# Second attention: strides of four query blocks instead of two, one score matmul per head and block, all value products as 64-column tiles

## The chip, the cores and the metric

The kernel runs on one core of a Trainium2 chip. The metric is the time of one execution on the device, in microseconds (us). A run's time is the median of several executions. TensorE (PE) multiplies matrices and writes to PSUM, eight banks of 128 partitions x 512 float32. VectorE (DVE) and ScalarE (ACT) read PSUM and write SBUF; GpSimd (POOL) works on SBUF alone; SyncE (SP) issues the DMAs. Each engine takes its instructions in the order in which they are written, and they meet through semaphores.

## What is computed

Two layers on x of 4 x 1024 tokens x 256. Each is `x + attention(layernorm(x)) * silu(ffn(layernorm(x)))`. The change is in the attention of the second layer alone:

```python
NUM_HEADS, HEAD_DIM, WINDOW, GLOBAL_HEADS = 32, 64, 128, 2
q, k, v = (xn @ W.T, split in 32 heads of 64)           # Wq, Wk, Wv: 2048 x 256
q, k = q * cos + rotate_half(q) * sin, k * cos + rotate_half(k) * sin
# heads 0 to 29, for each block of 128 queries that begins at `start`
ks = max(0, start - 64)
s = q[start:start+128] @ k[ks:start+128].T / 8          # causal mask, softmax
out = softmax(s) @ v[ks:start+128]
# heads 30 and 31: the same over all keys up to the query
return out @ Wo.T + bo
```

So a block of 128 queries of a local head looks at its own 128 keys and at the 64 keys before them: 192 columns of scores, 128 for the first block of a sequence.

## The kernel before, in words

The program has four stages: `first_half`, `first_attention`, `gate_network` and `second_attention`. The last is the one that is changed; in the trace it begins at about 1705 us. All its matmuls are float32 or fp32r.

**Turns and strides.** Two heads lie on 128 partitions, 64 each, and are worked on together in a *turn*; 4 sequences x 16 head pairs are 64 turns. 60 of them are local; the last of each 16 is *whole* (heads 30 and 31, all keys). A local turn has 8 query blocks and goes in 4 *strides* of two blocks; a whole turn has 8 strides of one block. `second_attention_plan` writes one list of steps, `plan`, and every engine walks through it and emits its own part of each step. The order of the list is therefore the order of each engine's instructions.

**The steps of a stride** and the letters used for them here:

- **S** (`first`): PE makes the scores into banks 0 to 3. The two heads use the upper and the lower 64 rows of the array. DVE adds the mask, writes SBUF (`pp`) and takes the row minimum of the negated scores (`nm`), one operation for each block and head; ACT then takes the exponential of each (`b_pp<-b_pp,b_nm`) with its sum.
- `second`: DVE takes the reciprocals of the sums, POOL multiplies the weights by them (`b_pp<-b_pp,b_rc`).
- **T** (`third`): PE transposes the weights of one block, three tiles of 128x128, into a bank; DVE copies them to `pt`, for blocks 1 and 5 ACT does.
- **W** (`fourth`): PE multiplies values by weights into bank 7; after four blocks ACT copies the bank to `oT`.

Before, S of stride s comes with W of stride s-3, `second` of s-1 and T of s-2. For one block the key layout is head 0: own 128 keys, earlier 64 keys; head 1: earlier 64, own 128. So head 0 takes two score matmuls (L1666 and L1669) and head 1 one of 192 columns (L1668). The two sets of 64 earlier keys make one transposed tile together. W is then one full-width matmul with a block-diagonal `vb` of the earlier values of both heads (L1717), and two 64-column matmuls, one a head, with the own values (L1722).

**Work for later turns** lies between: **P** (`proj`), 4 a turn, projects q or k for 512 tokens of the next turn (six 512-column matmuls; ACT copies to `qf`); `cos`, `sin`, `add` make the rotary embedding on DVE and POOL, with the rotated half fetched by DMA; **V** (`values`), 4 a turn, makes 128 tokens of values for the next pair of turns (six 256-column matmuls; ACT copies to `vv`). `w_high` and `v_high` are ACT copies of weights, once a turn and once in two turns. **O** (`out`) is the output projection of 128 tokens (eight records of 256 columns, L1731); DVE adds it to `acc`. Two O's fall in a local turn.

**Banks.** P, T, V and O take banks 4, 5, 6 in rotation, in the order of the plan. So each of them waits until the step three places before it in that order has been read out: T of a stride's second block, the fourth in the row P, T, V, T, waits for ACT's copy of P.

A float32 matmul of the program shows in the trace as two records; transposes and fp32r matmuls show as one.

Of the kernel before, what the change touches and what calls it, by code (L numbers as in the profile page):

```python
# [1234 lines left out]
def second_attention_plan():  # L1235
# [6 lines left out]
    def work(n):  # L1242
# [16 lines left out]
        if 2 * m < NTURN:  # L1259
            for i in range(4):  # L1260

                slot = 2 * i + 1 if n % NP or n == 0 else 5 + i // 2 * 2
                out[slot].append(("values", m, n % 2 * 4 + i))
# [14 lines left out]
    def end(at):  # L1278

        out = [[], [], [], []]  # L1280
        if 0 <= at - 3 < len(strides):
            out[0] = [("fourth", at - 3)]
        if 0 <= at - 1 < len(strides):
            out[1] = [("second", at - 1)]
        if 0 <= at - 2 < len(strides):
            out[2], out[3] = [("third", at - 2, 0)], [("third", at - 2, 1)]
        return out

    for n in range(NTURN):
# [13 lines left out]
        for j in range(8 if last else 4):  # L1303
            strides.append((n, j if last else 2 * j))
            s = len(strides) - 1
            a, c = (slots[j], []) if last else (slots[2 * j], slots[2 * j + 1])
            e = end(s)
            p += [("first", s)] + e[0] + e[1] + a + e[2] + c + e[3]
            if store:
                p.append(store.pop())  # L1310
            if side and s % 2:
                p.append(side.pop(0))
                if p[-1][1] % 4 == 3:
                    store.append(("store", *p[-1][1:]))
# [3 lines left out]
    for s in range(len(strides), len(strides) + 3):  # L1318
        p += [x for y in end(s) for x in y]
# [5 lines left out]
def second_attention(nc, A, M, X, out):  # L1325
    with ExitStack() as ctx:
# [14 lines left out]
        def counts(s):  # L1341

            return 4 * s - 2 * sum(whole(n) for n, _ in strides[:s])
# [3 lines left out]
        slot_of, slot_users, pt_of, pt_end = {}, [], {}, {}  # L1347
        for s in plan:
# [3 lines left out]
            elif s[0] == "first":  # L1352
                n, i = strides[s[1]]

                read = (nm_ready, counts(s[1] + 1))
                if whole(n) and i >= 4:
# [5 lines left out]
                slot_of[s[1]] = [len(slot_users) + h for h in range(2 if whole(n) else 1)]  # L1362
                slot_users += [s[1]] * len(slot_of[s[1]])
# [17 lines left out]
        mk = sb("mk", [128, L + 64])  # L1381
# [8 lines left out]
        qf = [sb(f"qf{i}", [128, L]) for i in range(2)]  # L1390
        rt = [sb(f"rt{i}", [128, L]) for i in range(2)]
        qk = [[sb(f"{n}p{i}", [128, L]) for i in range(2)] for n in "qk"]
        vv = [sb(f"vv{i}", [128, NQ, 256]) for i in range(2)]
        vb = [sb(f"vb{i}", [128, NQ - 1, 128]) for i in range(2)]
        pp = [sb(f"pp{i}", [128, L]) for i in range(6)]
# [4 lines left out]
        nm = [sb(f"nm{i}", [128, 4]) for i in range(4)]  # L1400
        sm = [sb(f"sm{i}", [128, 4]) for i in range(4)]
        rc = [sb(f"rc{i}", [128, 4]) for i in range(4)]
# [5 lines left out]
        rt_in = [[sem(f"rt_in{i}{h}") for h in range(2)] for i in range(2)]  # L1408
# [13 lines left out]
        sins = {s[1:]: i + 1 for i, s in enumerate(s for s in plan if s[0] == "sin")}  # L1422

# [3 lines left out]
        def third_done(s):  # L1427

            return P.filled(("third", s, 1, pieces(s, 1) - 1))

        def n_sums(s):
            return 2 if whole(strides[s][0]) else 4

        def weights(s, u, h):


            lo, hi = span(strides[s][1] + u, h)
            return pp[slot_of[s][0] % 6][:, 384 * u + lo:384 * u + hi]

        def span(i, h):  # L1440

            return (192 * h + (0 if i else 64 * h), 192 * h + (192 if i else 128 + 64 * h))
# [8 lines left out]
        def sync(e):  # L1451
# [7 lines left out]
            w.wait_ge(set_up, 1)  # L1459
            e.dma_start(mk[:, L - 128:L], A["mask"]).then_inc(c_in, 16)  # L1460
            for s in plan:
# [17 lines left out]
                elif k == "earlier":  # L1479
                    v = vv[n // 2 % 2]  # L1480
                    w.wait_ge(*P.emptied(("values", n // 2, NQ - 1)))
                    w.wait_ge(set_up, 5)
                    if n >= 2:
                        w.wait_ge(pv_done, pt_end[vb_before(n)])
                    for h in range(2):
                        at = n % 2 * 128 + 64 * h
# [442 lines left out]
```

## Time and profile before

| | us |
|---|---|
| median of 3 runs | 3341.18 |
| the runs | 3335.10, 3341.83, 3341.18 |
| profiled execution | 3339.75 |
| its span, first to last instruction | 3338.0 |
| share of the span: PE / PE weight load / DVE / ACT / POOL busy | 96 / 68 / 67 / 58 / 38% |

How to read the rows further below. A row of the timeline has the start in us, the time in us, the engine, the line of the kernel, the operation and what it writes and reads. Neighbouring rows of one kind are merged, with their count. Matmuls overlap: the time of one row runs on past the start of the next. What a step takes on PE is therefore the difference of two *starts*. "[1.35 <-ACT b_qf L1583]" is idle time ahead of the row, and what ended it. PEclk is the granted TensorE clock as a share of 2.4 GHz.

### The profile page before, as it was taken

Reading aid. Unit: us, or ns where it says so; the run is one execution under the profiler, and the core shown is the slowest. Engines: PE = TensorE matmul, PEld = TensorE weight load, DVE = VectorE, ACT = ScalarE, POOL = GpSimd, SP = SyncE. Lnnn points to the kernel's source line nnn. Section 1 sums busy time; section 2 is a strip of 40 time slices with the busy share of each in tenths; the row PEclk is TensorE's granted clock in tenths of the full one; section 3 lists DMA queues with packets and bytes.
Section 4 is the critical chain, followed back from the end, with each engine's and each line's share of the span. In section 5 each row is a group of like instructions: output and inputs, shape, how many; then the busy total and the mean of one; then the engine's idle time right before and its main releaser. Section 6 shows DMA issues by size and latency. Waiting matters only on the chain. (4 is left out here: it accounts for less than half of the span.)

```text
span 3338.0 us, 62439 instructions
## 1 busy us (share of the span) xinstructions
PE 3210.2 (96%) x21286; PEld 2270.4 (68%) x21286; DVE 2234.2 (67%) x6694; ACT 1952.7 (58%) x4806; POOL 1275.7 (38%) x1689
## 2 busy tenths in 40 slices
PE   7999999979999999996989999999999999999998
PEld 5888888812333333324877887788877888788886
DVE  6777666569888888866755555665556655665556
ACT  4666666637767667773446555455555555555553
POOL 1111111010000000002037776677766777667773
PEclk9999999979999999998999999999999999999999
DMA  4111111042113122103133333333333333233322
GB/s 136 43 44 39 43 46 37 7 82 64 40 30 68 40 56 46 27 6 125 67 115 85 76 75 95 86 89 82 76 83 98 91 73 82 70 93 79 82 69 62
DMA packets 246877, 225.88 MB, mean 68 GB/s; under 512 B 87392, under 2 KB 193184, under 8 KB 246432
## 3 DMA queue, kind: packets, MB, share of 16 engines
q1 hardware_dynamic: 246560, 221.89, 26.3%
q8 instruction: 171, 2.80, 0.4%
q14 instruction: 146, 1.20, 0.1%
HBM read 100.65 MB, written 39.85 MB: 42 GB/s over the span
## 5 line engine op out<-in xcount | busy, mean ns | idle before, releaser
L1555 POOL TENSOR_SCALAR b_pp<-b_pp,b_rc 128x128 f32<-128x128 f32 x960 | 592.3, 634 | 407.1 <-DVE b_rc L1791 405.1
L1598 ACT ACTIVATE b_pp<-b_pp,b_nm 128x128 f32<-128x128 f32 x960 | 419.3, 438 | 479.6 <-DVE b_nm L1782 479.5
L903 DVE TENSOR_REDUCE a_mx<-ps 128x1 f32<-128x512 f32 x1024 | 636.5, 681 | 86.9 <-PE ps L851 86.8
L825 ACT ACTIVATE a_pt<-ps 128x512 f32<-128x512 f32 x1024 | 534.8, 601 | 243.8 <-PE ps L862 242.3
L1782 DVE CUSTOM_DVE_ANT_0 b_pp<-ps,b_mk 128x128 f32<-128x128 f32 x960 | 277.7, 345 | 235.6 <-PE ps L1669 235.1
L851 PE MATMUL ps<-a_k,a_q 96*128 96x512 bf16 x1024 | 399.0, 391 | 18.9 <-DMA a_k<-qk_parts 16.1
L862 PE MATMUL ps<-a_q,a_k 99*128 99x512 bf16 x1024 | 387.0, 382 | 8.9 <-issue 5.4
L1803 DVE COPY b_pt<-ps 128x384 f32<-128x384 f32 (+3 forms) x456 | 240.0, 538 | 221.4 <-PE ps L1693 201.0
L638 DVE SCALAR_TENSOR_TENSOR f_yac<-ps,f_cw,f_yac 128x128 f32<-128x128 f32 x992 | 276.7, 343 | 122.1 <-PE ps L447 120.6
L1542 POOL TENSOR_TENSOR b_rt<-b_rt,b_sin 128x512 f32<-128x512 f32 x256 | 325.6, 1272 | 12.4 <-DMA b_rt<-b_qf 12.1
L851 PEld LDWEIGHTS ps<-a_k,a_q 96*128 96x128 bf16 x1024 | 100.0, 98 | 291.2 <-issue 150.9
L447 PEld LDWEIGHTS ps<-w,f_sq 128*128 128x128 f32 x2048 | 264.9, 191 | 29.6 <-DVE f_yac L638 7.2
L872 PE MATMUL ps<-a_pt,a_v 128*32 128x512 f32 x2048 | 272.8, 604 | 0.0
L447 PE MATMUL ps<-w,f_sq 128*128 128x128 f32 x2048 | 270.2, 275 | 1.5 <-DVE f_yac L638 0.3
L1731 PE MATMUL ps<-b_wo,b_oT 128*128 128x256 f32 x1024 | 242.2, 380 | 4.5 <-ACT b_vv L1578 4.5
L1693 PE MATMUL ps<-ident,b_pp 128*128 128x128 f32 x1380 | 229.4, 274 | 3.1 <-ACT b_qf L1583 2.0
L805 POOL CAST a_n<-a_nr 16x128 bf16<-16x128 f32 x32 | 9.0, 280 | 529.3 <-DVE a_nr L920 529.3
L1666 PE MATMUL ps<-b_kp,b_qp 64*128 64x128 f32 x960 | 209.1, 308 | 0.1
L1731 PEld LDWEIGHTS ps<-b_wo,b_oT 128*128 128x128 f32 x1024 | 185.1, 190 | 26.7 <-ACT b_vv L1578 5.2
L354 ACT ACTIVATE f_rl<-ps 128x512 f32<-128x512 f32 x256 | 152.0, 594 | 77.1 <-PE ps L105 73.0
L1693 PEld LDWEIGHTS ps<-ident,b_pp 128*128 128x128 f32 x1380 | 168.9, 141 | 37.8 <-issue 4.3
L1668 PE MATMUL ps<-b_kp,b_qp 64*128 64x192 f32 x840 | 194.5, 346 | 0.0
(257 smaller groups left out, 7110.6 us busy)
## 6 DMA issues: line engine op xcount, KB each, us to landing
b_rt<-b_qf SPq DMA_DIRECT2D x1024, 64.0 KB, 2.0
b_vb<-b_vv SPq DMA_DIRECT2D x120, 112.0 KB, 2.6
qk_parts<-f_aa SPq DMA_DIRECT2D x32, 384.0 KB, 2.6
a_q<-qk_parts SPq DMA_DIRECT2D x192, 64.0 KB, 3.0
a_k<-qk_parts SPq DMA_DIRECT2D x96, 128.0 KB, 5.2
v_rows<-f_va_ SPq DMA_DIRECT2D x16, 512.0 KB, 3.0
a_v<-v_rows SPq DMA_DIRECT2D x4, 2048.0 KB, 11.5
b_raw<-in_W1qT SPq DMA_DIRECT2D x64, 128.0 KB, 2.6
```

Of the source, the lines that this page charges most:

```text
L447: m = e.matmul(P.ap(s)[:, i * 128:(i + 1) * 128], sq[d % 4][:, i * 128:(i + 1) * 128], M["w2"][:, s[2], :], start=True, stop=True)
L638: m = e.scalar_tensor_tensor(out=o, in0=src, scalar=by, in1=o, op0=ALU.mult, op1=ALU.add)
L825: e.activation(pt[(4 * i + j) % 8][:, :], P.ap(s), ACT.Exp).then_inc(P.free_sem(s), 1)
L851: e.matmul(P.ap(s), q6[u % 3][0:KS, half, j, t * 128:(t + 1) * 128], k6[u % 3][0:KS, j, h * CH:(h + 1) * CH], start=True, stop=True).then_ ...
L862: e.matmul(P.ap(s), k6[u % 3][:, j, c * 128:(c + 1) * 128], q6[u % 3][:, h, j, :], start=True, stop=True).then_inc(P.full_sem(s), 1)
L903: e.tensor_reduce(mx[kh % 3][:, j * 4 + t, h:h + 1], P.ap(s), AX.X, ALU.max, negate=True).then_inc(P.free_sem(s), 1)
L1542: e.tensor_tensor(rt[x][:, t], rt[x][:, t], sin[:, t], ALU.mult).then_inc(sin_done, 1)
L1555: m = e.tensor_scalar(x, x, r[:, 2 * u + h:2 * u + h + 1], 1.0, ALU.mult, ALU.mult)
L1598: e.activation(x, x, ACT.Exp, bias=nm[n % 4][:, c:c + 1], scale=-1.0, accum_out=sm[n % 4][:, c:c + 1]).then_inc(exp_done, 1)
L1693: m = e.transpose(P.ap(f)[:, c * 128:(c + 1) * 128], x[:, at:at + 128], ident[:, :])
L1731: m = e.matmul(P.ap(s)[:, 0:256], oT[:, n % 2 * 4 + c, t * 128:(t + 1) * 128], wo[n % 2][:, c, :], start=c == 0, stop=c == 3)
L1782: m = e.tensor_tensor_reduce(out=weights(n, u, h), in0=ps[:, at + h, 192 * (u - h) + lo:192 * (u - h) + hi], in1=mk[:, L - 128 - 256 * h + ...
```

## The change

Strides of a local turn have four blocks, so there are two a turn. In the list, a stride is now: `second` of s-1, S of s, W of s-2, then two of the four exponential steps of s (a step is the two heads of a block), then four slots of P, V and rotary work; after each slot comes, as long as there are any, an exponential step and T of one block of s-1. W of a stride thus comes two strides after its S, not three.

- S: keys get 64 columns of zeros ahead (`kp` is 64 + 1024 wide), and each head and block has one score matmul of 192 columns, the first block of a sequence too, with a mask `mk0` that hides its first 64. S takes banks 0 to 3 at once. DVE and ACT work on 192 columns everywhere.
- Layout: a block's 384 weights are head 0 (64 earlier keys, 128 own) and head 1 (the same). The three transposed tiles hold: head 0's earlier 64 and its first 64 own; head 0's last 64 own and head 1's earlier 64; head 1's own 128. Values are laid out to match by four DMAs a turn (before two): `vs` and `vb`, both zero where a row belongs to the other head.
- W: four 64-column matmuls a block, two a head; no full-width matmul is left in it.
- `qf` is two buffers of 512 columns (before 1024), `rt` three of 512 (two of 1024), and `pp` three of 2048 (six of 1024).
- Whole turns keep strides of one block; their W lies three strides behind S as before, and T two.

```diff
-            p += [("first", s)] + e[0] + e[1] + a + e[2] + c + e[3]
+    def stride(s, slots):
+        out, turned = [("second", s - 1)] if s else [], []
+        if s < len(strides):
+            out.append(("first", s))
+        if 1 <= s:
+            if local(s - 1):
...
+                else:
+                    out += fourths(s - 1)
+                turned = thirds(s - 1)
...
+        exps = [("exp", s, u) for u in range(n_exp)] if mine else []
+        out += exps[:2]
+        exps = exps[2:]
+        for u in range(max(len(slots), len(turned))):
+            if u < len(slots):
+                out += slots[u]
+            if exps:
+                out.append(exps.pop(0))
+            if u < len(turned):
+                out.append(turned[u])
+        return out
```

```diff
 # PE, "first" of a local turn
-                        for u in range(2):
-                            d, c = 128 * (i + u), 192 * u
-                            lo = max(0, d - 64)
-                            q0, q1 = q[0:64, d:d + 128], q[64:128, d:d + 128]
-                            s0, s1 = ps[:, at, c:c + 192], ps[:, at + 1, c:c + 192]
-                            e.matmul(s0[:, 0:128], q0, kk[0:64, d:d + 128], start=True, stop=True)
-                            if d:
-                                m = e.matmul(s1, q1, kk[64:128, lo:d + 128], start=True, stop=True)
-                                m = e.matmul(s0[:, 128:192], q0, kk[0:64, lo:d], start=True, stop=True)
-                            else:
-                                m = e.matmul(s1[:, 64:192], q1, kk[64:128, 0:128], start=True, stop=True)
+                        for u in range(4):
+                            d = 128 * (i + u)
+                            for h in range(2):
+                                r = slice(64 * h, 64 * h + 64)
+                                m = e.matmul(scores(u, h), q[r, d:d + 128], kk[r, d:d + 192], start=True, stop=True)
```

```diff
 # PE, "fourth" of a local turn
-                                e.matmul(P.ap(o)[:, at], vb[vb_of(t) % 2][:, i + u - 1, :],
-                                         pt[pt_of[n, u, 0] % 5][:, 0, :], start=u == 0 or i == 0, stop=False)
...
-                                m = e.matmul(P.ap(o)[64 * h:64 * h + 64, at],
-                                             v[:, i + u, right + 64 * h:right + 64 * h + 64],
-                                             pt[pt_of[n, u, 0] % 5][:, 1 + h, :], start=False, stop=u == 1)
...
+                            e.matmul(o0, vs[x][:, i + u, :], y[:, 0, :], start=u == 0, stop=False)
+                            e.matmul(o1, v[:, i + u, right + 64:right + 128], y[:, 2, :], start=u == 0, stop=False)
+                            e.matmul(o0, vb[x][:, i + u, 0:64], y[:, 1, :], start=False, stop=u == 3)
+                            e.matmul(o1, vb[x][:, i + u, 64:128], y[:, 1, :], start=False, stop=u == 3).then_inc(pv_done, 1)
```

What stands in a row on PE before, from one stride of a local turn: its scores (S), its value products (W) and the start of P. `b_kp` and `b_qp` are keys and queries, `b_pt` the transposed weights.

```order
L1666 MATMUL ps<-b_kp,b_qp 128x128 [waits b_k_add,b_q_add,b_nm]
L1668 MATMUL ps<-b_kp,b_qp 128x192
L1669 MATMUL ps<-b_kp,b_qp 128x64
L1666 MATMUL ps<-b_kp,b_qp 128x128
L1668 MATMUL ps<-b_kp,b_qp 128x192
L1669 MATMUL ps<-b_kp,b_qp 128x64
L1717 MATMUL ps<-b_pt,b_vb 128x128
L1717 MATMUL ps<-b_pt,b_vb 128x128 [waits bank4_free]
L1722 MATMUL ps<-b_pt,b_vv 64x128 x4
```

The same place now: the end of the stride before (O), S, and the first of four blocks of W.

```order
L1764 MATMUL ps<-b_wo,b_oT 128x256 x3
L1709 MATMUL ps<-b_kp,b_qp 128x192 [waits b_k_add,b_q_add,b_nm]
L1709 MATMUL ps<-b_kp,b_qp 128x192 x7
L1755 MATMUL ps<-b_pt,b_vs 64x128
L1756 MATMUL ps<-b_pt,b_vv 64x128
L1757 MATMUL ps<-b_pt,b_vb 64x128
L1758 MATMUL ps<-b_pt,b_vb 64x128
```

S went from six matmuls of three widths for two blocks to eight of one width for four, and the change from full-width to 64-column matmuls inside W is gone.

ACT before, one and a half strides: `b_oT` is the copy of W's bank, `b_qf` of P, `b_vv` of V, `b_pt` of T; the rows with `b_pp` are the exponentials.

```order
L1598 ACTIVATE b_pp,b_sm<-b_pp,b_nm 128x128 [waits b_nm,b_rc]
L1598 ACTIVATE b_pp,b_sm<-b_pp,b_nm 128x128 [waits b_nm]
L1598 ACTIVATE b_pp,b_sm<-b_pp,b_nm 128x192 [waits b_nm] x2
L1615 ACTIVATE b_oT<-ps 128x512 [waits b_pv]
L1583 ACTIVATE b_qf<-ps 128x512 [waits b_q_add,bank4_full]
L1578 ACTIVATE b_vv<-ps 128x256 [waits bank6_full]
L1606 ACTIVATE b_pt<-ps 128x384 [waits bank4_full]
L1598 ACTIVATE b_pp,b_sm<-b_pp,b_nm 128x192 [waits b_nm,b_rc]
```

ACT now, one stride and the head of the next:

```order
L1641 ACTIVATE b_pp,b_sm<-b_pp,b_nm 128x192 [waits b_nm,b_rc]
L1641 ACTIVATE b_pp,b_sm<-b_pp,b_nm 128x192 [waits b_nm] x3
L1634 ACTIVATE b_qf<-ps 128x512 [waits b_rt_in2,b_cos,bank4_full]
L1641 ACTIVATE b_pp,b_sm<-b_pp,b_nm 128x192 [waits b_nm] x2
L1627 ACTIVATE b_vv<-ps 128x256 [waits bank6_full]
L1641 ACTIVATE b_pp,b_sm<-b_pp,b_nm 128x192 [waits b_nm] x2
L1649 ACTIVATE b_pt<-ps 128x384 [waits bank4_full]
L1634 ACTIVATE b_qf<-ps 128x512 [waits b_rt_in0,b_cos,bank5_full]
L1627 ACTIVATE b_vv<-ps 128x256 [waits bank4_full]
L1658 ACTIVATE b_oT<-ps 128x512 [waits b_pv]
```

The copy of W's bank (`b_oT`, with a wait for the end of W, `b_pv`) stood behind a stride's exponentials; now it stands ahead of them, and four of eight exponentials stand between the copies of P, V and T.

PE now, the second half of a stride (T of its second block stands ahead of these rows, in the bank that P had):

```order
L1730 MATMUL ps<-ident,b_pp 128x128 [waits bank5_free,b_norm]
L1730 MATMUL ps<-ident,b_pp 128x128 x2
L103 MATMUL ps<-b_vh,xh 128x256 [waits bank6_free]
L104 MATMUL ps<-b_vl,xh 128x256
L105 MATMUL ps<-b_vh,xl 128x256
L103 MATMUL ps<-b_vh,xh 128x256
L104 MATMUL ps<-b_vl,xh 128x256
L105 MATMUL ps<-b_vh,xl 128x256
L1730 MATMUL ps<-ident,b_pp 128x128 [waits bank4_free,b_norm]
L1730 MATMUL ps<-ident,b_pp 128x128 x2
L1764 MATMUL ps<-b_wo,b_oT 128x256 [waits bank7_free,b_wo_in0,bank5_free]
```

The row of a full stride on PE is now S, W, P, T, V, T, P, T, V, T, O. With three banks in rotation the second T waits for ACT's copy of the first P (bank 6 in this stride), and the second V for ACT's copy of the second T (bank 6 again).

## Rows read from the trace of the kernel before

**Rows 1.** Busy time by stretch: us; busy of each engine; PEclk, DMA share, GB/s.

```profile
1705.00:3338.00 1633.00, 1601.69 (x12052) 1312.07 (x12052) 979.03 (x3485) 901.16 (x2905) 1100.18 (x1472) 0.99 0.34 84
2021.54:2045.34 23.80, 23.80 (x181) 19.80 (x180) 13.83 (x52) 14.05 (x46) 17.61 (x24) 1.00 0.29 66
```

**Rows 2.** Timeline of PE, first rows of each step of a local stride.

```profile
2002.72 0.37 PE L1666 MATMUL ps<-b_kp,b_qp 64*128 64x128 f32 x1
...
2003.76 0.71 PE L1717 MATMUL ps<-b_pt,b_vb 128*128 128x128 f32 x4
...
2004.99 0.50 PE L103 MATMUL ps<-xh,b_wh 128*128 128x512 f32 x1
...
2006.48 0.49 PE L1693 MATMUL ps<-ident,b_pp 128*128 128x128 f32 x3
2006.73 0.36 PE L103 MATMUL ps<-b_vh,xh 128*128 128x256 f32 x1
...
2007.52 0.49 PE L1693 MATMUL ps<-ident,b_pp 128*128 128x128 f32 x3
2007.85 1.89 PE L1731 MATMUL ps<-b_wo,b_oT 128*128 128x256 f32 x8
2009.67 0.37 PE L1666 MATMUL ps<-b_kp,b_qp 64*128 64x128 f32 x1
```

**Rows 3.** Timeline of PE, scores of whole turns and what follows them.

```profile
2475.97 0.70 PE L1658 MATMUL ps<-b_kp,b_qp 64*128 64x256 f32 x4
2476.60 0.86 PE L1717 MATMUL ps<-b_pt,b_vb 128*128 128x128 f32 x4
...
2485.24 1.13 PE L1658 MATMUL ps<-b_kp,b_qp 64*128 64x512 f32 x4
2486.30 0.44 PE L1707 MATMUL ps<-b_pt,b_vv 128*64 128x128 f32 x4
```

**Rows 4.** Timeline of PE, the longest value product of a whole turn.

```profile
2528.32 1.97 PE L1707 MATMUL ps<-b_pt,b_vv 128*64 128x128 f32 x32
2530.21 0.50 PE L103 MATMUL ps<-xh,b_wh 128*128 128x512 f32 x1
```

**Rows 5.** Groups of weight loads (PEld), 2526.5 to 2530.3 us: count, busy us, mean ns.

```profile
L1707 PEld LDWEIGHTS ps<-b_pt,b_vv 128*64 128x64 f32 x32 | 1.7, 137 | 0.1
```

**Rows 6.** Timeline of ACT, back-to-back operations in local and whole turns.

```profile
2006.68 0.60 ACT L1583 ACTIVATE b_qf<-ps 128x512 f32<-128x512 f32 x1 [0.49 <-PE ps L105]
2007.17 0.63 ACT L1566 ACTIVATE b_wh<-b_raw 128x512 fp32r<-128x512 f32 x1
...
2011.73 0.44 ACT L1598 ACTIVATE b_pp<-b_pp,b_nm 128x192 f32<-128x192 f32 x1
...
2012.61 0.44 ACT L1598 ACTIVATE b_pp<-b_pp,b_nm 128x192 f32<-128x192 f32 x1
...
2025.76 0.62 ACT L1571 ACTIVATE b_vh<-b_vraw 128x512 fp32r<-128x512 f32 x1
2026.30 0.38 ACT L1578 ACTIVATE b_vv<-ps 128x256 f32<-128x256 f32 x1
2026.63 0.49 ACT L1606 ACTIVATE b_pt<-ps 128x384 f32<-128x384 f32 x1
```

**Rows 7.** Timeline, ACT copies in a whole turn and PE waiting for them.

```profile
2489.15 0.36 ACT L1578 ACTIVATE b_vv<-ps 128x256 f32<-128x256 f32 x1
2489.57 0.70 PE L1731 MATMUL ps<-b_wo,b_oT 128*128 128x256 f32 x2 [1.49 <-ACT b_vv L1578]
...
2504.76 0.57 ACT L1615 ACTIVATE b_oT<-ps 128x512 f32<-128x512 f32 x1
2505.24 0.58 ACT L1583 ACTIVATE b_qf<-ps 128x512 f32<-128x512 f32 x1
...
2505.97 0.63 PE L1683 MATMUL ps<-ident,b_pp 128*128 128x128 f32 x4 [1.35 <-ACT b_qf L1583]
```

**Rows 8.** Timeline of POOL, one local stride.

```profile
2012.20 2.49 POOL L1555 TENSOR_SCALAR b_pp<-b_pp,b_rc 128x192 f32<-128x192 f32 x4 [3.32 <-DVE b_rc L1791]
```

More of the change, by code:

```diff
@@ L1276, in second_attention_plan, with local, fourths, thirds @@
     side, store = [], []
[L1278 to L1286, printed above, removed]
+    def local(s):
+        return strides[s][0] % NP != NP - 1
+    done = 0
+    def fourths(upto):
+        nonlocal done
+        out = [("fourth", s) for s in range(done, upto)]
+        done = max(done, upto)
+        return out
+    def thirds(s):
+        return [("third", s, u) for u in range(4 if local(s) else 2)]
+    def stride(s, slots):
[4 more added lines that the diff above has]
+            if local(s - 1):
+                if s >= 2 and not local(s - 2):
+                    out += fourths(s - 2) + thirds(s - 2)
+                    out += fourths(s - 1)
+                else:
+                    out += fourths(s - 1)
+                turned = thirds(s - 1)
+            else:
+                out += fourths(s - 2)
+                if s >= 2 and not local(s - 2):
+                    turned = thirds(s - 2)
+        mine = s < len(strides)
+        n_exp = 4 if mine and local(s) else 2
+        exps = [("exp", s, u) for u in range(n_exp)] if mine else []
[8 more added lines that the diff above has]
+                out.append(turned[u])
         return out
@@ L1302, in second_attention_plan @@
         slots = work(n)
-        for j in range(8 if last else 4):
-            strides.append((n, j if last else 2 * j))
+        for j in range(8 if last else 2):
+            strides.append((n, j if last else 4 * j))
             s = len(strides) - 1
-            a, c = (slots[j], []) if last else (slots[2 * j], slots[2 * j + 1])
-            e = end(s)
-            p += [("first", s)] + e[0] + e[1] + a + e[2] + c + e[3]
+            p += stride(s, [slots[j]] if last else slots[4 * j:4 * j + 4])
             if store:
                 p.append(store.pop())
-            if side and s % 2:
+            if side and (not last or j % 2):
                 p.append(side.pop(0))
@@ L1317, in second_attention_plan @@
             side += [("out", n // 4, t) for t in range(NQ)]
-    for s in range(len(strides), len(strides) + 3):
-        p += [x for y in end(s) for x in y]
+    s = len(strides)
+    p += [("second", s - 1)] + fourths(s - 2) + thirds(s - 2) + fourths(s - 1) + thirds(s - 1) + fourths(s)
     for s in side:
@@ L1339, in pieces @@
             return 1 + i // 4 if whole(n) else 1
-        def counts(s):
-            return 4 * s - 2 * sum(whole(n) for n, _ in strides[:s])
+        parts = [0]
+        for n, _ in strides:
+            parts.append(parts[-1] + (2 if whole(n) else 4))
+        sums = [0]
+        for n, _ in strides:
+            sums.append(sums[-1] + (2 if whole(n) else 8))
         nm_ready = sem("nm")
         n_t = n_misc = n_pair = 0
-        slot_of, slot_users, pt_of, pt_end = {}, [], {}, {}
+        pt_of, pt_end = {}, {}
         for s in plan:
@@ L1353, in second_attention @@
                 n, i = strides[s[1]]
-                read = (nm_ready, counts(s[1] + 1))
-                if whole(n) and i >= 4:
+                read = (nm_ready, sums[s[1] + 1])
+                if not whole(n) or i >= 4:
                     P.take(s, 0, 1, 2, 3, by=read)
@@ L1778, in vector @@
                     else:
[L1779 removed]
+                        for u in range(4):
                             for h in range(2):
[L1781 removed]
+                                mask = mk[:, L - 192:L] if i + u else mk0[:, :]
                                 m = e.tensor_tensor_reduce(
[L1783 to L1784 removed]
+                                    out=weights(n, u, h), in0=scores(u, h), in1=mask, scale=-0.125, scalar=3e38,
                                     op0=ALU.add, op1=ALU.min, accum_out=nm[n % 4][:, 2 * u + h:2 * u + h + 1])
```

192 lines of the change are left out of this document (94 added, 98 removed).

## The prediction

> **What bounds the kernel now.** I read the busy times by stretch first [rows 1]. In the last stage, the only one that is touched, PE is busy 1601.69 of 1633.00 us. One local turn takes 23.80 us, with PE busy for all 23.80 of them, at full granted clock; ACT is busy 14.05, DVE 13.83, POOL 17.61. So the local turns, 60 of 64, are a pure queue on PE. What an edit is worth there is what it takes off PE's row of steps, unless another engine then comes late. Then I read PE's timeline by the differences of starts [rows 2]: S (two blocks) 2003.76 - 2002.72 = 1.04, W (two blocks) 1.23, P behind W 1.49, T between P and V 0.25, V 0.79, the other T 0.33, O 1.82. The busy times alone would mislead, since matmuls overlap. Last I read ACT [rows 6, 7] and POOL [rows 8], because the change reorders them.
>
> **PE's part, step by step.** All in us, for one local turn.
>
> S. Two heads run at once in the two halves of the rows, and a block has two passes. A whole turn shows what equal pairs cost: two pair passes of 256 columns take 2476.60 - 2475.97 = 0.63, two of 512 columns 1.06 [rows 3]. So 512 more columns in all cost 0.43, 0.84 ns a column, and 0.20 is fixed: the switch into and out of this shape. Four blocks of 192 columns are eight pair passes: 8 x 0.161 + 0.20 = 1.49, twice a turn 2.98. Before it is 4 x 1.04 = 4.16, less some 0.22 for the first block with 128 columns (6 x 192 and 2 x 64 fewer columns; I scale by the same 0.84 ns and allow for the missing matmul): 3.94. Gain 0.96. It comes half from halving the switches, half from the uneven widths, which leave one half of the array idle in turns.
>
> W. 32 records of 64-column tiles took 2530.21 - 2528.32 = 1.89, with a switch on either side [rows 4]. After the change W of four blocks is just that: 16 pairs. Twice a turn 3.78. Before it is 4 x 1.23 = 4.92, less 0.22 for the first block, which has no earlier keys: 4.70. Gain 0.92.
>
> P. Behind W it takes 1.49, since its first matmul pays a switch; V, all regular, shows some 0.10 less for this. Two of four P's now stand behind T: gain 0.20. T. The first block has a third tile to transpose: 0.11 lost. V, O: nothing. The switch from T or O into S is paid twice fewer: about 0.09 each, gain 0.18. Sum: 0.96 + 0.92 + 0.20 + 0.18 - 0.11 = 2.15. A stride with nothing in the way is 1.49 + 1.89 + 1.49 + 0.25 + 0.79 + 0.33 + 1.39 + 0.25 + 0.79 + 0.33 + 1.82 = 10.82, the turn 21.64, against 23.80. Over 60 turns that would be 130 us.
>
> A rule speaks against the pairs of W. What the rows show: 32 weight loads of the longest W average 137 ns and lie in a step of 1.89 us [rows 4, 5]; in line they alone would be 4.4, so they overlap. The Trainium skill, TensorE: Matmul & The Clock Gate, Part 3, says that a weight load overlaps with matmuls in flight only when its row group differs, and tiles of 64 columns over all 128 rows share theirs. By that, the 16 more pairs of a turn would each add a load: 16 x 0.137 = 2.2, and the gain on PE would be gone, whatever ACT does (it is a rival below).
>
> **ACT's part.** I walk through a full stride from PE's first S. At 1.49 + 1.89 = 3.38 W is done. ACT's next instruction is the copy of W's bank, which waits for exactly this; the stride's eight exponentials are queued behind it, though DVE has their data from about 2 on. Behind them in turn stand the copies that PE needs to get its banks back. By the starts of back-to-back rows: the `oT` copy holds ACT 0.48 [rows 7], an exponential 0.44, the `qf` copy 0.49, the `vh` copy 0.54; the `vv` copy is 0.38 long and, by the 0.1 by which its neighbours overlap, holds it 0.29; the `pt` copy ends 0.49 after its start [rows 6]. The unknown is how soon ACT starts after W; I take 0.10.
>
> - `oT` starts 3.48, four exponentials from 3.96, `qf` of P from 5.72, done 6.32.
> - The second T needs that bank. PE is ready at 3.38 + 1.49 + 0.25 + 0.79 = 5.91. It restarts 0.15 after such a copy with two waits (2505.24 + 0.58 to 2505.97) and 0.06 after one with one (2489.15 + 0.36 to 2489.57) [rows 7]: 6.47. PE loses 0.56.
> - Two exponentials, `vv`, two exponentials, then the `pt` copy of that T: 5.72 + 0.49 + 0.88 + 0.29 + 0.88 = 8.26, done 8.75.
> - The second V needs this bank. PE, past T and P, is ready at 6.47 + 0.33 + 1.39 + 0.25 = 8.44 and starts at 8.80. PE loses 0.36.
> - V 0.79, T 0.33, O 1.82: the stride ends at 11.74.
>
> Two strides are 23.48. Once in two turns `v_high` stands between `qf` and the exponentials: 0.54, in the mean 0.27 a turn. So 23.75 against 23.80: the 2.15 that PE saves go almost wholly into its waits for ACT. It is one rigid loop: PE's W releases ACT, ACT's copies release PE, and only what stands in the loop counts. A longer W moves the end one for one, the first P and V not at all.
>
> What else could be late, and isn't. POOL: four multiplications in 2.49 [rows 8], so eight in at most 5.0, from 0.7 in the stride, where DVE has the reciprocals; T of block u then has its weights at 0.7 + 1.25(u + 1), and PE reaches it at 4.9, 6.5, 8.2, 9.6. The `sin` work ends well before the next stride. DVE: eight evictions behind S, then rotary work, then the first T's copy by about 6.0, where P needs that bank at 6.8. The two more DMAs a turn for the values are issued more than a stride ahead of their W. Each of these is costed at nothing; if DVE's cover went, P would move and with it nothing up to 8.4, so 0.3 are free there too.
>
> Whole turns keep their steps and their waits; in them and in the turn behind them the gain of S and the new waits about cancel too, within 1 us a sequence. The first two turns run before any W holds ACT up; I take the gain of S there, 2 us. Sum: 60 x 0.05 + 2 = 5 off 3339.75 for the profiled execution, which stands 1.4 below the median: **3336**.
>
> **The bounds.** Two sizes in the loop are uncertain: ACT's start after W, 0 to 0.2, and PE's restart at V, 0.06 to 0.15. With the rounding of nine exponentials and copies that is 0.2 a stride either way, 24 us in all: 3312 to 3360.
>
> **Rivals.**
>
> (a) ACT isn't late: PE's whole gain comes through, 3341 - 130 = 3211. For it speaks that ACT is busy only 14 of 23.8 us. Against it: the copies stand behind a wait in one queue, and the bank rotation gives PE no way round.
>
> (b) Slower: ACT loses the overlap of neighbours. The page shows each operation 0.1 longer than the distance to the next one's start. In the loop there are five changes of kind (`oT` to exponential, to `qf`, to exponential, to `vv`, to exponential and `pt`), several with two or three semaphores to wait for, where before there was one. If each costs the 0.1, a stride is 0.5 longer: 120 x 0.5 = 60, 3396. It decides from 0.1 a stride on (the time then is slower by over 0.2%). Against it: the waits are met long before, as in the row from 2006.68 to 2007.17 [rows 6].
>
> (c) The loads of W stand in line as in the rule above. W is in the loop, so 8 more pairs a stride by 0.137 come in full: 120 x 1.1 = 132 on top of 3336, 3468. Against it are [rows 4, 5].
>
> (d) The change isn't what it says, for instance pairs of 192 columns don't run at once. Whole turns have the same pairs at other widths [rows 3], so this has next to no chance.
>
> **Chances.** The forecast 0.80, (a) 0.07, (b) 0.10, (c) and (d) 0.03. Within 0.2% of 3341.18 means 3334.5 to 3347.9, about what a measurement can tell from no change. Within the forecast's bounds, centred on 3336, I give faster 0.43, same 0.35, slower 0.22. Faster: 0.80 x 0.43 + 0.07 = 0.41. Same: 0.28. Slower: 0.80 x 0.22 + 0.13 = 0.31. The range 3312 to 3362 leaves out (a), (c) and most of (b). The single likeliest time lies at the edge of "faster", and I hold neither sign for shown.
>
> **What would show it.** In the trace of the changed kernel: local turns of 23.5 to 23.8 us, those with `v_high` half a microsecond longer. S of four blocks 1.49, W 1.89 from start to start; if these are right, PE's sum is right. PE idle in nearly every full stride ahead of the second T, released by ACT's `qf` copy, and ahead of the second V, released by ACT's `pt` copy; together 0.9 of start-to-start time, of which the trace shows less as idle, as its rows run on. ACT idle from its last `vv` to the end of W, then busy without a gap. The forecast is wrong if ACT starts its exponentials before W ends, or if PE waits for POOL or DVE: then a cover above was thinner than I read it.

## The result: slower, by 2.45%

| | us |
|---|---|
| changed kernel, median of 4 runs | 3420.36 (3414.88 to 3427.57) |
| kernel before, median of 4 runs beside them | 3339.72 (3335.10 to 3341.83) |
| ratio, 95% interval | 1.0245 (1.0222 to 1.0267) |
| span of the profiled execution, after / before | 3418.9 / 3338.0 |

The forecast was 3336, its range ended at 3362. The time is 84 us above the one and 58 above the other. The stages ahead of the last one are as they were.

I read the profile after in the order of the prediction. First the busy times by stretch, as [rows 1]: the last stage, then four local strides (half a turn each), then two pieces of the last of these. The columns are the stretch, its length, the busy time of PE, PE's weight loads, DVE, ACT and POOL, then PEclk, DMA share and GB/s.

```profile
1705.00:3338.00 1633.00, 1496.91 (x11825) 1228.06 (x11826) 1120.63 (x3239) 831.98 (x2832) 921.93 (x1436) 0.97 0.38 91
2222.30:2234.05 11.75, 11.28 (x93) 9.37 (x92) 9.06 (x27) 6.09 (x22) 8.98 (x12) 1.00 0.30 78
2015.79:2027.56 11.77, 11.38 (x93) 9.41 (x92) 8.07 (x25) 6.69 (x23) 5.25 (x10) 1.00 0.79 177
2245.81:2258.77 12.96, 11.29 (x93) 9.38 (x92) 9.46 (x25) 6.20 (x22) 7.84 (x13) 1.00 0.22 54
2001.27:2015.79 14.52, 12.87 (x93) 10.57 (x92) 9.45 (x25) 6.20 (x22) 7.14 (x13) 0.88 0.16 36
2007.00:2009.60 2.60, 0.95 (x8) 0.53 (x6) 2.60 (x4) 2.60 (x13) 0.86 (x2) 1.00 0.16 39
2009.80:2013.10 3.30, 3.30 (x11) 2.61 (x11) 0.97 (x3) 0.79 (x2) 1.27 (x1) 0.50 0.17 40
```

A stride that goes well takes 11.75, or 12.28 where ACT has `v_high` in it. Two of them make a turn of 23.5 or 24.05, in the mean 23.8: the forecast said 23.75. But some strides take 12.96 and some 14.52. So the question is not why the turn is longer than I summed. It is what happens in *some* strides.

The waits of PE answer half of it (waiting line, who released it, us in total, times, longest):

```profile
PE ps L103 <- DVE b_pt L1835: 49.5, 39, 1.3
PE ps L1730 <- ACT b_qf L1634: 42.5, 108, 0.4
PE ps L103 <- ACT b_pt L1649: 12.7, 27, 0.6
```

The second and third are the two waits for ACT that the forecast walked through. The first is new: 39 times PE waits 1.27 us, ahead of P, for DVE's copy of the first T's bank. Why is that copy late? The instructions that write K, on DVE, give it away (count: shortest/median/longest in ns, first and last start). Of before, then of after:

```profile
L1754 DVE TENSOR_TENSOR b_kp<-b_qf,b_cos x128: 656/661/693, 1716.9 to 3277.0; 128x512 f32<-128x512 f32 x128
```

```profile
L1787 DVE TENSOR_TENSOR b_kp<-b_qf,b_cos x128: 685/1926/3317, 1717.1 to 3356.3; 128x512 f32<-128x512 f32 x128
```

The same product (K by its cosines, `cos` in the plan) on the same 128x512 values takes 0.66 us before, and up to 3.32 after. I call it K's product from here. It stands between the evictions and the copy of the first T. The timelines of DVE and POOL show what lies beside it. First in the stride that takes 14.52:

```profile
2005.11 3.30 DVE L1787 TENSOR_TENSOR b_kp<-b_qf,b_cos 128x512 f32<-128x512 f32 x1
2008.34 0.68 DVE L1793 TENSOR_TENSOR b_qp<-b_qp,b_rt 128x512 f32<-128x512 f32 x1
2008.94 0.55 DVE L1835 COPY b_pt<-ps 128x384 f32<-128x384 f32 x1
```

```profile
2004.40 0.83 POOL L1604 TENSOR_SCALAR b_pp<-b_pp,b_rc 128x192 f32<-128x192 f32 x2
2005.20 1.29 POOL L1591 TENSOR_TENSOR b_rt<-b_rt,b_sin 128x512 f32<-128x512 f32 x1
2006.44 1.42 POOL L1579 TENSOR_TENSOR b_wl<-b_raw,b_wh 128x256 fp32r<-128x256 f32 x2
```

Then in one that takes 11.75:

```profile
2226.14 0.78 DVE L1787 TENSOR_TENSOR b_kp<-b_qf,b_cos 128x512 f32<-128x512 f32 x1
2226.84 0.68 DVE L1793 TENSOR_TENSOR b_qp<-b_qp,b_rt 128x512 f32<-128x512 f32 x1
```

```profile
2225.16 2.98 POOL L1604 TENSOR_SCALAR b_pp<-b_pp,b_rc 128x192 f32<-128x192 f32 x5
2228.10 1.27 POOL L1591 TENSOR_TENSOR b_rt<-b_rt,b_sin 128x512 f32<-128x512 f32 x1
```

I say that DVE *asks* for an instruction where its row starts. In the bad stride DVE asks for K's product at 2005.11, and POOL's sine product starts at 2005.20. K's product then lasts until POOL's sine product and both low halves are through (2006.44 + 1.42 = 2007.86) and needs its own 0.5 or so after that. In the good stride POOL is still at its multiplications by a scalar when DVE asks. There POOL is the one that waits: five multiplications take 2.98 where two others took 0.83. Where such instructions meet, only one of the two engines works at a time, and the one that lost waits for more than one instruction of the other.

The Trainium skill, SBUF — State Buffer, section on who interferes with whom, states this lock: a VectorE instruction with two SBUF inputs and a GpSimd instruction that reads SBUF exclude each other, and whoever is first keeps the shared port for the whole instruction. The rows agree that one blocks the other. They do not fit what the page says of the first one: DVE asks while POOL's last multiplication is still running (to 2004.40 + 0.83 = 2005.23), 0.09 us ahead of the sine product, and then waits not for that one instruction but for the three behind it.

That leaves the strides of 14.52. PE's wait in them is 1.27, as in the ones of 12.96. The rest is TensorE's clock. After PE had been busy for 0.95 of 2.60 us, its granted clock fell to 0.50, which is the 1.2 GHz level, for some 3.4 us; the P of that time took 2.60 us from start to start (2009.54 to 2012.14) against 1.46 in a good stride (2205.02 to 2206.48).

```profile
2007.75 0.52 PE L1730 MATMUL ps<-ident,b_pp 128*128 128x128 f32 x3 [0.38 <-ACT b_qf L1634]
2009.54 0.67 PE L103 MATMUL ps<-xh,b_wh 128*128 128x512 f32 x1 [1.27 <-DVE b_pt L1835]
...
2012.14 0.84 PE L1730 MATMUL ps<-ident,b_pp 128*128 128x128 f32 x3
```

I counted all 39 strides with a product of 3.3 us by the starts of their scores in the trace: 18 take 13.0, 1.2 more than a good one; 21 take 14.5, 2.8 more. 18 x 1.2 + 21 x 2.8 = 80 of the 84 us. The strides whose product takes 1.93 (the sine product alone in the way; 41 of them, without those behind a whole turn) take 11.75 or 12.28 like the good ones, the last two 10.93: so much of a delay P's slack still covers.

Whether a stride is bad follows from where POOL's multiplications lie. In each of the 39, DVE takes the reciprocals 0.45 into the stride, POOL's eight multiplications run from 0.74 to 3.97, the sine product follows at 3.93, and DVE asks for K's product at 3.85. The good strides from 2162 to 2246 are the first ones behind a whole turn, and likewise those from 2584 and 3003. There DVE has two more instructions for each finished output block (the multiplication by the gate and the addition of x, `b_gx`). They put the reciprocals off to 1.37 and the multiplications to 1.66, so that K's product meets a multiplication. The 41 strides with 1.93 lie like the 39, but are first strides of a turn, where no low halves follow the sine product. DVE and POOL in the stride from 2222.30, then in the first bad one, from 2245.81:

```profile
2222.86 0.42 DVE L1851 TENSOR_TENSOR b_acc<-b_acc,b_gx 128x256 f32<-128x256 f32 x1
2223.32 0.42 DVE L1853 TENSOR_TENSOR b_acc<-b_acc,b_gx 128x256 f32<-128x256 f32 x1
2223.66 0.19 DVE L1823 RECIPROCAL b_rc<-b_sm 128x8 f32<-128x8 f32 x1
2223.96 4.18 POOL L1604 TENSOR_SCALAR b_pp<-b_pp,b_rc 128x192 f32<-128x192 f32 x8 [1.69 <-DVE b_rc L1823]
```

```profile
2246.26 0.19 DVE L1823 RECIPROCAL b_rc<-b_sm 128x8 f32<-128x8 f32 x1
2246.55 3.22 POOL L1604 TENSOR_SCALAR b_pp<-b_pp,b_rc 128x192 f32<-128x192 f32 x8
```

### The profile page after: what moved, and what is told of

Same layout as the page of the kernel before. It is cut to its first block, busy times and chain, and to the rows that moved or that the text cites. A ratio compares the mean times of both kernels' runs of the same rounds, so it can differ in the third digit from the quotient of the medians.

```text
span 3418.9 us, 62597 instructions
## 1 busy us (share of the span) xinstructions
PE 3173.3 (93%) x21586; PEld 2237.3 (65%) x21586; DVE 2427.4 (71%) x6577; ACT 1908.4 (56%) x4806; POOL 1122.3 (33%) x1689
## 4 chain that ended last, share of the span: by engine, by line
PE 29%; ACT 9%; DVE 7%; issue 3%; DMA 1%; POOL 1%; SPq 1%; ACTq 0%; DVEq 0%
ACT b_pp L1641 7%; PE ps L1764 6%; PE ps L1709 5%; DVE b_kp L1787 4%; PE ps L103 3%; PE ps L1755 3%; PE ps L1730 3%; PE ps L1757 2%; PE ps L105 2%; PE ps L104 2%; DVE b_pp L1814 2%; ACT b_qf L1634 1%; PE ps L1702 1%; DVE b_pt L1835 1%; ACT b_pt L1649 1%
## 5 line engine op out<-in xcount | busy, mean ns | idle before, releaser
L1641 ACT ACTIVATE b_pp<-b_pp,b_nm 128x192 f32<-128x192 f32 (+2 forms) x1024 | 473.0, 466 | 59.2 <-DVE b_nm L1806 49.9
L1604 POOL TENSOR_SCALAR b_pp<-b_pp,b_rc 128x192 f32<-128x192 f32 x960 | 420.3, 459 | 189.1 <-DVE b_rc L1823 188.8
L1658 ACT ACTIVATE b_oT<-ps 128x512 f32<-128x512 f32 x128 | 76.5, 598 | 630.0 <-PE ps L1758 586.3
L1835 DVE COPY b_pt<-ps 128x384 f32<-128x384 f32 (+3 forms) x456 | 247.0, 553 | 226.8 <-PE ps L1730 210.0
L1814 DVE CUSTOM_DVE_ANT_0 b_pp<-ps,b_mk 128x192 f32<-128x192 f32 x960 | 276.2, 353 | 93.8 <-PE ps L1709 92.7
L1730 PE MATMUL ps<-ident,b_pp 128*128 128x128 f32 x1440 | 248.7, 284 | 52.8 <-ACT b_qf L1634 42.5
L1787 DVE TENSOR_TENSOR b_kp<-b_qf,b_cos 128x512 f32<-128x512 f32 x128 | 250.1, 1954 | 3.3 <-ACT b_qf L1634 3.3
L1730 PEld LDWEIGHTS ps<-ident,b_pp 128*128 128x128 f32 x1440 | 181.0, 146 | 108.9 <-issue 56.4
L1641 ACT ACTIVATION_READ_ACCUMULATOR b_pp<-b_pp,b_nm 128x1 f32 x1024 | 196.2, 192 | 0.0
```

The lines of the kernel that those rows point to most:

```text
L1604: m = e.tensor_scalar(x, x, r[:, 2 * u + h:2 * u + h + 1], 1.0, ALU.mult, ALU.mult)
L1641: e.activation(x, x, ACT.Exp, bias=nm[n % 4][:, c:c + 1], scale=-1.0, accum_out=sm[n % 4][:, c:c + 1]).then_inc(exp_done, 1)
L1730: m = e.transpose(P.ap(f)[:, c * 128:(c + 1) * 128], pp[n % 3][:, at:at + 128], ident[:, :])
L1787: e.tensor_tensor(qk[x][n % 2][:, t], qf[proj_of[s[1:]] % 2][:, :], cos[:, t], ALU.mult).then_inc(cos_done, 1)
L1814: m = e.tensor_tensor_reduce(out=weights(n, u, h), in0=scores(u, h), in1=mask, scale=-0.125, scalar=3e38, op0=ALU.add, op1=ALU.min, accum_ ...
```

## The experiments

"LOCK" is this theory: K's product meets POOL's two-operand work (instructions that read two tiles), holds the first T's copy, and PE loses 1.27 us and often its clock. The rivals were ACT (its loop is dearer than I summed it) and DMA (the added value transfers delay the others). ACT's order was to be tested as well, since the forecast says that it eats PE's gain.

### K's product ahead of the evictions

```diff
         out, turned = [("second", s - 1)] if s else [], []
+        if s < len(strides) and local(s):
+            for x in [x for x in slots[0] if x[0] == "cos"]:
+                slots[0].remove(x)
+                out.append(x)
         if s < len(strides):
             out.append(("first", s))
```

> One edit to the changed kernel: in local strides VectorE takes K's cosine product ahead of the evictions instead of behind them; all work stays. Theory LOCK: the 84 us above my forecast (3420 against 3336) come from this product, which takes 1.93 or 3.31 us instead of 0.68 where it meets GpSimd's sine product and low halves, and holds the first T's copy behind it. Then the product falls to under 0.8 us, TensorE's wait of 49.5 us for b_pt L1835 goes, and the time is 3336 (3325 to 3350). Rival ACT: the excess is ScalarE's loop, dearer than I summed it; then the time stays within 10 us of 3420. Rival DMA: the added value transfers delay what VectorE and GpSimd wait for; the time stays at 3420 as well.

Measured: 3344.41 (3341.30 to 3346.90, 10 runs), 1.0013 of before (1.0004 to 1.0023). That is 76 us off the changed kernel by the order of one instruction on DVE. K's product in this trace, then PE's first waits in the last stage:

```profile
L1791 DVE TENSOR_TENSOR b_kp<-b_qf,b_cos x128: 639/640/1695, 1718.0 to 3277.8; 128x512 f32<-128x512 f32 x128
```

```profile
PE ps L1734 <- ACT b_qf L1638: 43.0, 109, 0.4
PE ps L103 <- ACT b_pt L1653: 15.9, 27, 0.6
```

The wait for DVE's copy is gone, and what is left are the forecast's own two. Behind the first few, and apart from those that follow a whole turn, the local turns all take 23.5 or 24.05. ACT and DMA as causes of the excess fall: neither was touched.

### The T copy ahead of K's product

```diff
+        if mine and local(s) and turned:
+            moved = [x for x in slots[0] if x[0] in ("cos", "add")]
+            slots[0] = [x for x in slots[0] if x[0] not in ("cos", "add")]
+            slots[1] = moved + slots[1]
         for u in range(max(len(slots), len(turned))):
```

> One edit to the changed kernel: in local strides the two or three cosine and addition products of the first slot stand behind the first T's copy on VectorE, not ahead of it. The meeting with GpSimd stays or moves, but the T copy no longer stands behind it. If the path of the loss is product -> T copy -> bank -> P, the wait for b_pt L1835 goes and the time falls to 3336 to 3350. If the loss ran through the product's own result (ScalarE's qf buffer, the addition), it stays at 3400 or more.

Measured: 3348.11 (3346.83 to 3352.02), 1.0029 (1.0017 to 1.0041). PE's wait ahead of P for the first T's copy is gone. The product now stands 2 us later and meets POOL less often: 71 of 128 products are under 0.9 us, 14 over 1.6. Where it is long, something is still lost, ahead of O, whose bank the third T's copy gives back. One such product, then PE's row:

```profile
2208.98 2.17 DVE L1791 TENSOR_TENSOR b_kp<-b_qf,b_cos 128x512 f32<-128x512 f32 x1
```

```profile
2213.48 1.99 PE L1768 MATMUL ps<-b_wo,b_oT 128*128 128x256 f32 x8 [0.31 <-DVE b_pt L1839]
```

The nine strides with 2.17, none with `v_high` in it, take 12.31 to 12.33 where 11.76 is the good time, and two with 2.65 take 12.80. So the loss of the changed kernel runs through the copy behind the product: with the first T's copy ahead of it that loss is gone, and what a long product still costs here comes through the next copy behind it. For K itself PE waits three times, 2.9 us in all.

### GpSimd's low halves two slots later

```diff
-            out[5] += [("w_low", n + 2, 0), ("w_low", n + 2, 1)]
+            out[7] += [("w_low", n + 2, 0), ("w_low", n + 2, 1)]
```

> One edit to the changed kernel: GpSimd's two low halves of the next weights (1.42 us) stand two slots later, behind Q's sine product, so that in the second stride of a turn only the sine product (1.29 us) lies in K's cosine product's way. LOCK: the 3.31 us products become 1.93, the first strides' stay at 1.93, and the strides that end 2.8 us late end some 1.2 late: 3350 to 3395. ACT or DMA: unchanged, 3420 within 10.

Measured: 3343.97 (3341.62 to 3348.93), 1.0012 (1.0003 to 1.0022). Faster than I expected. I had counted a loss for products of 1.93 as well, and they cost nothing. No product takes 3.3 any more, as expected. The longest is 2.3:

```profile
L1787 DVE TENSOR_TENSOR b_kp<-b_qf,b_cos x128: 680/791/2265, 1717.7 to 3280.5; 128x512 f32<-128x512 f32 x128
```

The meeting itself has not gone: 52 of the 128 products still take 1.92 to 2.27, in the second strides of a turn above all, and nearly all these strides take 11.76 or 12.28 like the good ones. 71 are under 0.9. Most of these stand in first strides, where the low halves, now the last of POOL's work in a turn, put its multiplications off from 0.74 to some 1.1 into the stride. K's product then meets a multiplication. So it was the 1.42 us of the low halves in the product's way that made the meeting costly.

### One more instruction on GpSimd

If the rows are read rightly, what counts is which kind of POOL instruction comes next when DVE asks. These two kernels put one instruction that serves nothing between POOL's last multiplication and what follows, once in each local stride. The first:

```diff
                             m.then_inc(norm_done, 1)
+                        e.tensor_scalar(extra[:, :], mk[:, 0:160], r[:, 0:1], 1.0, ALU.mult, ALU.mult)
```

> The changed kernel with one more GpSimd instruction in each local stride and nothing else: a multiplication of 128x160 scratch values (some 0.35 us, it serves nothing) between the last multiplication of the weights and what follows, most often a sine product. In the slow strides VectorE asks for K's cosine product 0.09 us ahead of the sine product, and waits for all that GpSimd has next; in the free ones it asks 0.2 us ahead of a multiplication with a scalar, which waits for it. LOCK with that hand-over: the added instruction lets VectorE in ahead of the sine product, the product falls to under 0.9 us, and 0.35 us more work in 120 strides make the kernel some 70 us faster: 3340 to 3355. Rival, GpSimd is simply too late: more work there makes it slower by up to 120 x 0.35: 3420 to 3462.

The second:

```diff
+                        e.tensor_tensor(extra[:, 0:96], mk[:, 0:96], mk[:, 96:192], ALU.mult)
```

> As the run with one more GpSimd instruction in each local stride, at the same place and of about the same length, but of another kind: a product of two tiles of 128x96 (estimate 0.37 us from the rows of 128x256 in 0.72 and 128x512 in 1.29), not a multiplication of one tile by a scalar. If the kind of GpSimd's next instruction decides whether the waiting VectorE product gets in, the product now waits for this one too, and its row grows by up to 0.37: 3420 to 3465. If only the moment counts (any instruction there moves the sine product away from the hand-over), it does what the scalar one did: 3340 to 3355.

Measured: 3343.51 (3341.27 to 3351.71), 1.0010 (1.0000 to 1.0020) with the scalar form; 3453.39 (3448.81 to 3461.43), 1.0341 (1.0322 to 1.0361) with the two-tile form. More work of the one kind makes the changed kernel 77 us faster, of the other 33 us slower. The timelines of POOL and DVE, scalar form first:

```profile
2066.99 1.37 POOL L1607 TENSOR_SCALAR b_extra<-b_mk,b_rc 128x160 f32<-128x160 f32 x1
2068.32 1.28 POOL L1592 TENSOR_TENSOR b_rt<-b_rt,b_sin 128x512 f32<-128x512 f32 x1
```

```profile
2066.88 0.69 DVE L1789 TENSOR_TENSOR b_kp<-b_qf,b_cos 128x512 f32<-128x512 f32 x1
2067.49 0.69 DVE L1795 TENSOR_TENSOR b_qp<-b_qp,b_rt 128x512 f32<-128x512 f32 x1
```

Then the two-tile form:

```profile
2092.26 0.40 POOL L1607 TENSOR_TENSOR b_extra<-b_mk 128x96 f32<-128x96 f32 x1
2092.61 1.29 POOL L1592 TENSOR_TENSOR b_rt<-b_rt,b_sin 128x512 f32<-128x512 f32 x1
2093.85 1.42 POOL L1580 TENSOR_TENSOR b_wl<-b_raw,b_wh 128x256 fp32r<-128x256 f32 x2
```

```profile
2092.16 3.67 DVE L1789 TENSOR_TENSOR b_kp<-b_qf,b_cos 128x512 f32<-128x512 f32 x1
```

DVE asks 0.11 and 0.10 us ahead of the added instruction. The scalar one lets DVE in, and waits for K's product and for the addition behind it: 1.37 in all, where the shortest of its 120 rows takes 0.39. The two-tile one does not, nor do the three behind it, and the product lasts 3.67.

### ACT's exponentials ahead of its output copy

```diff
+        mine = s < len(strides)
+        n_exp = 4 if mine and local(s) else 2
+        exps = [("exp", s, u) for u in range(n_exp)] if mine else []
+        if mine and local(s):
+            out += exps[:2]
+            exps = exps[2:]
         if 1 <= s:
...
-        mine = s < len(strides)
-        n_exp = 4 if mine and local(s) else 2
-        exps = [("exp", s, u) for u in range(n_exp)] if mine else []
-        out += exps[:2]
-        exps = exps[2:]
+        if not (mine and local(s)):
+            out += exps[:2]
+            exps = exps[2:]
```

> One edit to the changed kernel: in local strides ScalarE takes the first four exponentials ahead of the output copy that waits for the value products, not behind it. My forecast's ScalarE loop says that TensorE's waits of 0.56 us for qf and 0.36 us for ScalarE's pt copy, in each stride, follow from that order. If it holds, TensorE's wait for b_qf L1634 (42.5 us) nearly goes; the time depends on whether VectorE still meets GpSimd: 3310 to 3420, with K's cosine product still the row that decides. If the loop isn't the order, the wait stays at about 42 us and the time at 3420.

Measured: 3374.44 (3370.44 to 3384.63), 1.0110 (1.0091 to 1.0129). The wait for `qf` is no longer among the first, and the wait for DVE's copy now heads the list:

```profile
PE ps L103 <- DVE b_pt L1839: 89.4, 78, 1.9
```

Good turns fall to 22.2 to 22.9, so the loop was ACT's order, as forecast. But P now comes earlier, and the slack that covered the 1.93 us products is used up: 78 strides wait instead of 39.

### Both moves together

> The edits of the two runs before together: in local strides K's cosine product stands ahead of the evictions on VectorE, and the first four exponentials ahead of the output copy on ScalarE. From the trace with the exponentials moved alone: its undisturbed turns take 22.2 to 22.86 us (mean 22.5) against 23.79 with the product moved alone. So with both, LOCK and the ScalarE loop being separate causes, 60 local turns give back 1.2 to 1.3 us each against 3344: 3270 (3260 to 3290). Rival: with ScalarE's wait gone, another engine's order comes last at once, and VectorE meets GpSimd in a new place (turns of 24.5): 3320 to 3350.

Measured: 3276.76 (3275.19 to 3278.45), 0.9806 of before (0.9791 to 0.9820). This beats both kernels. Turns take 22.2, or 22.7 with `v_high`. With both causes gone, PE's own steps can be read. Its timeline, with one row of ACT, and the whole stride:

```profile
2195.76 1.57 PE L1717 MATMUL ps<-b_kp,b_qp 64*128 64x192 f32 x16
2197.27 0.32 PE L1763 MATMUL ps<-b_pt,b_vs 128*64 128x128 f32 x1
...
2199.16 0.50 PE L103 MATMUL ps<-b_xh,b_wh 128*128 128x512 f32 x1
...
2201.95 0.48 PE L103 MATMUL ps<-b_xh,b_wh 128*128 128x512 f32 x1
...
2203.38 0.47 ACT L1657 ACTIVATE b_pt<-ps 128x384 f32<-128x384 f32 x1
2203.44 0.49 PE L1738 MATMUL ps<-ident,b_pp 128*128 128x128 f32 x3
2203.90 0.39 PE L103 MATMUL ps<-b_vh,b_xh 128*128 128x256 f32 x1
```

```profile
2195.76:2206.87 11.11, 11.11 (x93) 9.38 (x93) 7.75 (x27) 6.73 (x23) 6.05 (x10) 1.00 0.94 196
```

### `v_high` later, and K's addition

Both kernels add to the two moves. The first takes ACT's conversion of the value weights out of the middle of the exponentials:

```diff
-            out[0].append(("v_high", m + 1))
-            out[1].append(("v_low", m + 1, 0))
-            out[3].append(("v_low", m + 1, 1))
+            out[3].append(("v_high", m + 1))
+            out[5].append(("v_low", m + 1, 0))
+            out[7].append(("v_low", m + 1, 1))
```

> The kernel with both moves, and ScalarE's conversion of the value weights (v_high, 0.52 us) one slot group later: at the end of the stride's exponentials instead of in their middle, its low halves on GpSimd four slots later. My forecast gave v_high 0.27 us a turn, since it stands in ScalarE's loop. With both moves made TensorE still waits 27 times 0.5 us for ScalarE's pt copy, in the turns with v_high alone: 13.5 us in all. If that is v_high's place, the wait goes: 3277 - 13 = 3264 (3260 to 3270). Rival: GpSimd's low halves, now in the second stride beside the weights' own, hold VectorE up in turn: 3275 to 3290.

The second puts DVE's additions of K one slot later as well:

```diff
-                                   [(*k, 1), ("cos", n + 1, 0, 1), ("add", n + 1, 1, 0)], [("sin", n + 1, 0, 1)])):
+                                   [(*k, 1), ("cos", n + 1, 0, 1)], [("sin", n + 1, 0, 1), ("add", n + 1, 1, 0)])):
...
-            late.append(([("cos", n + 1, 1, 1), ("add", n + 1, 0, 1)], [("sin", n + 1, 1, 1)], [("add", n + 1, 1, 1)]))
+            late.append(([("cos", n + 1, 1, 1), ("add", n + 1, 0, 1)], [("sin", n + 1, 1, 1)], [], [("add", n + 1, 1, 1)]))
```

> As the run before, with VectorE's addition of K behind the third T's copy too (it takes 1.22 us where it meets GpSimd, 0.69 alone, and the third copy stood behind it). The waits for VectorE's copies are already next to nothing in the trace with both moves, so by my theory this adds at most 2 us of gain: 3262 (3257 to 3268). If VectorE's place behind GpSimd still cost something unseen, 3255 or less.

Measured: 3260.95 (3255.66 to 3265.48), 0.9760 (0.9743 to 0.9776), and 3256.54 (3252.89 to 3259.39), 0.9751 (0.9737 to 0.9766). PE's wait for ACT's `pt` copy, 13.5 us with both moves, is gone with the first. The turns are nearly all 22.2. The second edit gave 4 us more where I expected 2 at most, but the two intervals overlap, so that these runs don't tell the two kernels apart.

## Why the prediction was wrong

- **PE's sum held, and proved a little low.** S of four blocks was put at 1.49 and W at 1.89. With both moves they take 1.51 (2197.27 - 2195.76) and 1.89 (2199.16 - 2197.27). The second P took 1.49 (2203.44 - 2201.95) where I had 1.39: also behind T a P takes as long as behind W. The whole stride with nothing in the way was to be 10.82 and is 11.11. But 0.2 of that is still a wait: V starts at 2203.90, 0.05 behind the end of ACT's `pt` copy (2203.38 + 0.47), 0.46 behind the T ahead of it, where the same step took 0.25 at 2200.66. That leaves some 10.9, an estimate from these rows, and 23.80 - 2 x 10.9 = 2.0 a turn off PE, where I had 2.15.
- **ACT's loop held.** Forecast were a stride of 11.74, with the second T at 6.47 and the second V at 8.80. In the good stride from 2198.25 they start 6.49 (2204.74) and 8.80 (2207.05) into it, and it takes 11.76. K's product moved alone gives 3344, 8 us above 3336 and in the range, so the rest of the forecast stands without the meeting. ACT's order moved as well gives back 68 us more (3276.76), 1.1 a turn of the 2.1 that I had ACT eat. With `v_high` later it is 83, or 1.4. So the order is a cause of these waits, but the two moves don't give back all that I had it eat.
- **The step that failed is the cover for DVE and POOL.** I wrote: "DVE: eight evictions behind S, then rotary work, then the first T's copy by about 6.0, where P needs that bank at 6.8. [...] Each of these is costed at nothing". In a good stride the copy does end at 6.0 (2227.71 + 0.56 in the stride from 2222.30). In the stride from 2001.27 it starts at 2008.94, 7.7 into the stride, and ends at 8.2, and PE waits 1.27 for it. I had summed DVE's rows by their lengths in the trace of before, as if POOL's work beside them did not matter.
- **The evidence lay in the rows that I used.** The row of [rows 8] has four multiplications in 2.49 us. Back to back they take about 0.40 each: in the changed kernel eight take 3.23. The rest of the 2.49 was the first one, 1.29 long in the trace, waiting for K's product on DVE and the addition behind it. I read it as a price of 0.62 each, called it an upper end ("at most 5.0"), and so put POOL's sine product 1.8 us later than it comes. With 5.0, K's product would have met a multiplication, which lets it in; with 3.23 it meets the sine product, by 0.09 us.
- **The sentence "P would move and with it nothing up to 8.4, so 0.3 are free there too"** was tried by 39 strides. P starts 8.27 into them, against 6.77 in a good one (2205.02 - 2198.25): 1.5 later, five times the 0.3. The sentence also left out that a wait can cost PE its clock: of the 80 us counted by stride, the 39 waits are 49.5, and the rest comes with the 21 strides in which the clock fell.
- **The rivals.** None was this one. (a), ACT not late, falls with PE's 108 waits for `qf`. (c), loads of W in line, is refuted by 1.89 for W: the trace disagrees with the rule of the Trainium skill that the prediction gives for it. (d), pairs that don't run at once, falls with 1.51 for S. (b), lost overlap on ACT, would have shown in the good turns and does not. The warning at the end ("if PE waits for POOL or DVE: then a cover above was thinner than I read it") named the right place without a price or a chance.

What stays open: why DVE, asking some 0.1 us ahead, loses to a two-tile instruction of POOL and wins against a scalar one. In both cases a multiplication of POOL is still running when it asks. The runs show that it does, not by what mechanism. And why 18 of the 39 equal waits left the clock at full and 21 did not: no run varied that.

## What to carry to other kernels

DVE and POOL cannot be costed by their separate rows: lay their timelines side by side, ask of each two-operand instruction what the other engine has next, and take a first instruction that is longer than its siblings as the sign of a meeting. Where a change moves either engine by a few tenths, price the stride with the meeting and without. And keep the copy that gives PE its bank back ahead of such an instruction, not behind it.

## What the runs showed of the hardware

- A two-operand DVE instruction of 0.66 us lasts up to 3.32 us beside three back-to-back two-operand instructions on POOL, and 3.67 beside four. It is not let in between them. The reverse holds as well: a POOL multiplication behind two such DVE instructions took 1.37 instead of 0.39.
- A POOL instruction with one tile and a scalar lets a waiting DVE product in, one with two tiles doesn't, at the same place within 0.1 us. The kernels differ by 110 us for it (3343.51 and 3453.39).
- DVE's evictions (from PSUM with a mask from SBUF) kept their 0.28 us from start to start beside POOL's multiplications (2004.56 to 2004.83 beside the row from 2004.40).
- A single wait of 1.27 us, behind a shorter one of 0.38, could send the granted clock from 1.00 to 0.50 for 3.4 us, and did 21 times of 39.
